# A fused two-layer kernel, its last chunk: pair 0 gated and row 1 turned earlier, pair 2's gates mixed by ScalarE and VectorE, and a third outer product on GpSimd

## The reference

```python
x = layernorm(x + L0_attn(x))
x = layernorm(x + L0_ffn(x))     # silu(x w1) * (x w2), two gelu layers of 1024, w3
x = layernorm(x + L1_attn(x))    # k, v, q = x W; k over its block norms; per step a state
                                 #   S = tanh(S + outer(v - S k, k)), out = f(S q), f(z) = z^2 sigmoid(z)
x = layernorm(x + L1_ffn(x))     # xr = mu_r x + (1 - mu_r) x_prev, xk likewise with mu_k
                                 #   out = sigmoid(xr W_r) * (relu(xk W_k)^2 W_v)
```

## Time and profile before

| | |
|---|---|
| timed runs, median | 1147.56 us |
| the profiled execution | 1148.24 us |
| its span in the profile | 1146.3 us |
| TensorE busy | 1096.8 us (96%) |
| VectorE busy | 954.2 us (83%) |
| ScalarE busy | 596.7 us (52%) |
| GpSimd busy | 516.8 us (45%) |

### The profile page before, as it was taken

One profiled execution on the slowest core, in us unless ns is written; L12 is line 12 of the kernel. 1 busy time (PEld: TensorE's weight loads), 2 busy tenths in 40 slices (PEclk: granted clock), 3 DMA queues, 4 the chain that ended last, 5 costly groups with the idle time before them and its releaser, 6 DMA issues.

```text
span 1146.3 us, 16623 instructions
## 1 busy us (share of the span) xinstructions
PE 1096.8 (96%) x5837; PEld 850.3 (74%) x5837; DVE 954.2 (83%) x1382; ACT 596.7 (52%) x1009; POOL 516.8 (45%) x426
## 2 busy tenths in 40 slices
PE   9999999999999999999999999999999999998386
PEld 5566666678787777788778887877887787886165
DVE  4798888882045998999899899989989998999886
ACT  2345555554446346645755574565557455644534
POOL 1477666774333244433424432443343344337852
PEclk9999999999999999999999999999999999999679
DMA  7246555523532430523134133314232330430001
GB/s 265 102 167 236 211 204 209 222 93 114 179 94 58 145 110 21 146 74 129 56 110 138 46 110 91 128 39 126 77 124 73 110 128 19 129 92 20 0 1 39
DMA packets 45114, 127.01 MB, mean 111 GB/s; under 512 B 4352, under 2 KB 21504, under 8 KB 43136
## 3 DMA queue, kind: packets, MB, share of 16 engines
q1 hardware_dynamic: 43904, 114.20, 31.5%
q10 hardware_dynamic: 1152, 12.07, 2.8%
HBM read 117.86 MB, written 19.92 MB: 120 GB/s over the span
## 4 chain that ended last, share of the span: by engine, by line
PE 77%; DVE 12%; POOL 6%; issue 3%; ACT 2%; POOLq 0%; DVEq 0%; ACTq 0%
PE lower L1257 46%; PE bank L1257 18%; PE lower L440 5%; PE lower L572 2%; POOL state L748 2%; POOL rgn L757 2%; PE bank L1246 1%; DVE y L847 1%; DVE y L852 1%; PE bank L487 1%; POOL a_lo L2017 1%; DVE tmp L2265 1%; PE lower L526 1%; PE lower L530 1%; PE bank L440 1%
## 5 line engine op out<-in xcount | busy, mean ns | idle before, releaser
L2017 POOL TENSOR_TENSOR a_lo<-whole,a_hi 128x512 fp32r<-128x512 f32 x128 | 181.9, 1438 | 267.0 <-ACT a_hi L1629 195.7
L1257 PE MATMUL lower<-b_hi,ring 128*128 128x512 f32 x512 | 193.6, 396 | 1.4 <-ACT a_hi L1629 1.4
L1257 PE MATMUL lower<-b_lo,ring 128*128 128x512 f32 x512 | 190.6, 390 | 1.7 <-POOL b_lo L2017 1.7
L1257 PE MATMUL lower<-a_hi,ring 128*128 128x512 f32 x496 | 186.3, 394 | 1.7 <-issue 1.7
L1257 PE MATMUL lower<-a_lo,ring 128*128 128x512 f32 x496 | 184.1, 389 | 0.3 <-POOL a_lo L2017 0.3
L2017 POOL TENSOR_TENSOR b_lo<-whole,b_hi 128x512 fp32r<-128x512 f32 x64 | 93.5, 1469 | 145.4 <-ACT b_hi L1629 145.4
L1612 ACT ACTIVATE S<-S 128x1024 f32<-128x1024 f32 x56 | 58.6, 1058 | 173.5 <-DVE S L2278 173.5
L1628 ACT ACTIVATE whole<-lower,hs 128x512 f32<-128x512 f32 x126 | 86.2, 685 | 79.3 <-PE lower L1257 77.3
L1257 PEld LDWEIGHTS lower<-b_hi,ring 128*128 128x128 f32 x512 | 96.2, 188 | 22.0 <-issue 1.8
L1257 PEld LDWEIGHTS lower<-b_lo,ring 128*128 128x128 f32 x512 | 96.0, 188 | 22.0 <-POOL b_lo L2017 2.3
L440 PE MATMUL lower<-wa,xT 128*128 128x512 f32 x240 | 109.5, 599 | 1.5 <-DVE turned L817 1.4
(11 more groups left out here) (302 smaller groups left out, 2398.9 us busy)
## 6 DMA issues: line engine op xcount, KB each, us to landing
ring<-ffn_copy_dram SPq DMA_DIRECT2D x128, 512.0 KB, 3.6
look<-ffn_dram ACTq DMA_DIRECT2D x6, 1879.0 KB, 6.9
ffn_copy_dram<-ffn_dram SPq DMA_DIRECT2D x4, 2112.0 KB, 11.4
rope<-rope_dram SPq DMA_DIRECT2D x8, 512.0 KB, 8.2
xtok<-x_dram SPq DMA_DIRECT2D x8, 512.0 KB, 4.2
x1in<-x_dram SPq DMA_DIRECT2D x8, 512.0 KB, 4.8
x1res<-x_dram SPq DMA_DIRECT2D x8, 512.0 KB, 3.3
xT<-xT_dram SPq DMA_DIRECT2D x7, 512.0 KB, 8.4
```

The source lines that it names most:

```text
L1257: ins = nc.tensor.matmul(out, a, b, start=(first and n == 0), stop=(last and n == len(pairs) - 1))
L2017: nc.gpsimd.tensor_tensor(lo[:, m, :], t["whole"][:, m % 4, :], hi[:, m, :].bitcast(F32), ALU.subtract).then_inc(lo_done, 1)
```

## The change

All of it is in the four `finish()` programs and their helpers.

- GpSimd takes a third outer product, that of s = 0. VectorE's `next_state(0, 1)` becomes `state_delta(0)`, then `scaled_keys(2, ...)`, then `state_added(0)`. `outer_product(0)` stands ahead of `read_q(0, 0)`; `mix_weights(3)` goes behind the reads of s = 0; `read_q(3, 0)` goes ahead of `added_mean(1)`.
- VectorE: `read_sums(0)` goes behind `next_state(1, 0)`, `mixed_pair(0)` ahead of `state_delta(2)`, `gate_rows(front)` ahead of `state_added(2)`, `mixed_pair(1)` behind `last_read(1)`. `update_sum` loses its reduce to `update_state` and, as `update_times`, goes behind the third of the rows.
- Pair 2's gates are made from mixed inputs (`mixed_gates`): two more copies on ScalarE, two more mixes on VectorE (`last_mix_inputs(0)`), four products instead of eight on TensorE.
- Rows: the fourth `last_down` goes ahead of `turn_row(0)`, ScalarE copies row 1 before its tanh, and `busy_while_waiting` runs six products at two places instead of eight at one.

```diff
-            READS = {(0, 0): 1, (0, 1): 2, (1, 0): 3, (1, 1): 4, (2, 0): 6, (2, 1): 7, (3, 0): 9}
-            OUTERS = {1: 5, 2: 8}
+            READS = {(0, 0): 2, (0, 1): 3, (1, 0): 4, (1, 1): 5, (2, 0): 7, (2, 1): 8, (3, 0): 10}
+            OUTERS = {0: 1, 1: 6, 2: 9}
...
+                        if g == 2:
+                            mixed_gates(n, gates, 1)
+                            return
...
+                    def mixed_gates(n, gates, mixed):
+
+                        pe.wait_ge(last_mixed, mixed)
+                        for r, b in enumerate(range(2 * n, 2 * n + 2)):
+                            ins = product(gates[:, r * DIM:r * DIM + DIM],
+                                          [(wide_b[:, k, b * P:b * P + P], wr[:, k, :]) for k in range(KD)])
+                        ins.then_inc(pair_dr, 1)
...
-                    for b in range(3):
+                    for b in range(BATCH):
                         last_down(b)
                     turn_row(0)
-                    last_down(3)
                     key_value_row(0)
                     query_row(0)
+                    pe.wait_ge(sig_done, 2 * LAST - 2)
+                    busy_while_waiting(bank[KEY_BANK[1]], 6)
...
-                    busy_while_waiting()
+                    pe.wait_ge(pair_sig, 2)
+                    busy_while_waiting(pair_banks(2)[1], 6)
...
                     x2_rows(1, range(1, BATCH))
+                    turned_row(1)
                     scan_tanh(d, BATCH - 1, 1)
-                    for b in range(1, BATCH):
+                    for b in range(2, BATCH):
                         turned_row(b)
...
+                    last_parts(2, 0)
                     key_acts(2, 0)
                     mix_gates(2, 0)
...
                     x2_root(1, slice(1, BATCH))
                     key_root(0, slice(0, 1))
-                    mix_weights(3)
                     key_root(1, slice(1, 2))
                     added_mean(0, every)
                     key_root(2, slice(2, BATCH))
                     added_root(0, every, t["rstd4"], t["shift4"])
+                    outer_product(0)
                     read_q(0, 0)
                     read_q(0, 1)
+                    mix_weights(3)
...
                     outer_product(2)
+                    read_q(3, 0)
                     added_mean(1, front)
-                    read_q(3, 0)
...
+                    ffn_row(1)
+                    ffn_row(2)
+                    update_times(d, 3, 1)
+                    ffn_row(3)
...
                     next_state(0, 0)
-                    next_state(0, 1)
+                    state_delta(0)
                     scaled_keys(2, slice(2, BATCH))
+                    state_added(0)
+                    next_state(1, 0)
                     read_sums(0)
-                    next_state(1, 0)
                     state_delta(1)
                     read_sums(1)
                     state_added(1)
                     next_state(2, 0)
+                    mixed_pair(0, 0)
                     state_delta(2)
                     read_sum(2, 0)
-                    mixed_pair(0, 0)
+                    gate_rows(front, 2, 1)
                     state_added(2)
-                    gate_rows(front, 2, 1)
-                    mixed_pair(1, 1)
                     read_sum(2, 1)
                     read_sum(3, 0)
                     last_read(1)
+                    mixed_pair(1, 1)
                     gate_rows(back, 6, 2)
+                    last_mix_inputs(0)
```

More of the change, by code:

```diff
@@ L1517, in last_products, with busy_while_waiting @@
                         ins.then_inc(pair_dk, 1)
-                        pe.wait_ge(last_mixed, 2)
                         pe.wait_ge(pair_gated, g)
-                        for r, b in enumerate(rows):
-                            ins = product(gates[:, r * DIM:r * DIM + DIM],
-                                          [(wide_b[:, k, b * P:b * P + P], wr[:, k, :]) for k in range(KD)])
-                        ins.then_inc(pair_dr, 1)
-                    def busy_while_waiting():
-                        pe.wait_ge(pair_sig, 2)
-                        for _ in range(8):
-                            nc.tensor.matmul(pair_banks(2)[1][:, 0:DIM], ident[:], wk[:, 0, :], start=True, stop=True)
+                        mixed_gates(n, gates, 3)
+                    def busy_while_waiting(unused, count):
+                        for _ in range(count):
+                            nc.tensor.matmul(unused[:, 0:DIM], ident[:], wk[:, 0, :], start=True, stop=True)
                     def pair_values(g, n):
@@ L1870, in last_parts @@
                         act.wait_ge(pair_dv, g - 1)
-                        for dst, nu in ((wide_a, nu_k), (wide_b, nu_r)):
+                        for dst, nu in ((wide_a, nu_k), (wide_b, nu_r))[3 - g:]:
                             for k in range(KD):
@@ L2104, in outer_product @@
                         pool.wait_ge(fin_times_k, DELTAS[s])
-                        if s == 2:
+                        if s:
                             pool.wait_ge(fin_pre, 2 * s + 2)
@@ L2255, in update, with update_times @@
                 def update(c, s, hf):
-                    update_sum(c, s, hf)
+                    update_times(c, s, hf)
                     update_state(s, hf)
-                def update_sum(c, s, hf):
+                def update_times(c, s, hf):
                     k, v, q, st, w = parts(s, hf)
-                    dl = delta[:, hf * HALF:hf * HALF + HALF, :]
                     dve.wait_ge(sq_done, c * 2 * BATCH + 2 * (s - 1) + hf + 1)
                     scan.done(nc.vector.tensor_tensor(w, st, along_j(k), ALU.mult))
-                    scan.wait()
-                    scan.done(nc.vector.tensor_reduce(dl, w, AX_X, ALU.add))
                 def update_state(s, hf):
@@ L2272, in update_state @@
                     dl = delta[:, hf * HALF:hf * HALF + HALF, :]
+                    scan.wait()
+                    scan.done(nc.vector.tensor_reduce(dl, w, AX_X, ALU.add))
                     scan.wait()
@@ L2569, in finish @@
                     row_moments(fin, t["mv2"], slice(0, 1), ve2)
-                    update_sum(d, 3, 1)
-                    for b in range(1, BATCH):
-                        ffn_row(b)
+                    ffn_row(1)
+                    ffn_row(2)
+                    update_times(d, 3, 1)
+                    ffn_row(3)
                     row_moments(fin, t["mv2"], slice(1, BATCH), ve2)
```

17 lines of the change are left out of this document (8 added, 9 removed).

## The result

The changed kernel took 1152.06 us (median of seven runs, 1150.85 to 1152.23) against 1147.56 (1147.28 to 1148.2): ratio 1.0037, interval 1.0027 to 1.0047. It is slower by 4.2 us by the ratio, 4.5 by the medians. The profiled executions took 1152.09 and 1148.24, with spans of 1150.3 and 1146.3. The last chunk begins 0.27 us later than before (`ffn_row(0)` at 1045.24 instead of 1044.97). No edit explains that; over the fourteen traces of this case `ffn_row(0)` starts between 1044.82 and 1045.38, so differences of this size are not counted as anybody's effect.

The account below looks back on a forecast made before the run. VectorE's chain of states bounds the last chunk to about 1115, then a relay of VectorE, ScalarE, GpSimd and TensorE. Back gates +2.7 and mixes +0.8 make +3.5, on the median 1147.56: 1151.1 us, range 1148.8 to 1154.0.

Parts of the forecast that it names:

- outer product ends: GpSimd's third outer product, started only after the fourth key root and added_root at 1081.77: ends 1083.8 to 1085.0, taken as 1084.5.
- back gates: Gates of pair 1's rows on VectorE, after last_read(1) and ScalarE's last gate parts: 1128.4 instead of 1125.74, +2.7 us.
- The lock: VectorE operation with two SBUF inputs and GpSimd operation reading SBUF exclude each other: the later starts when the earlier ends.
- The milder lock: Rival: front gates get their second turn before read (3,0), or first read ends before sums need it; -1.8, 1149.3; 12%.
- rivals without a lock: Rival: no lock at state_added(0) and the reads beside it; next_state(1, 0) starts at 1087.1, total 1144.0 us; 4%.
- fixed price of 0.6: Rival: each meeting of VectorE and GpSimd costs 0.6; four new meetings on the path, 2.4 us, total 1146.4; 4%.
- read_sums moved: Sums of step 0 placed behind next_state(1, 0): later GpSimd reads land on VectorE's operations, state_added(1) at 1104.7, +4.6 us.
- The rows: Row edits up to the start of step 1: -0.5 us, from 1074.16 to 1073.65; bounds 0 and 1.6.
- The half clock in rows 2 and 3: TensorE at 1.2 GHz in these rows after idling: ScalarE's sums, and with them GpSimd, up to 1.2 us later.
- Pair 2's gates: Two added mixes on VectorE's path cost +0.8 us; TensorE's saved 1.8 of 3.62 us is worth nothing, through at 1133.2.
- the slow clock: Rival: TensorE at 1.2 GHz at pair 2, keys up to 6.6 instead of 3.7 us, late by 2.2 to 3; 1153.7; 15%.
- 3.90 us wait: VectorE's wait before 1118.89 for TensorE's values of pair 1: goes away, giving back 2.6 us.

Follow-up runs that it names:

- short_reads: Changed kernel with GpSimd's two reads of step 0 cut to one block of sixteen each, all waits and signals kept: 1147.51 us, ratio 0.9999.
- one_input: Changed kernel with one SBUF operand of state_added(0) exchanged for the old contents of the PSUM array: 1150.41 us, ratio 1.0025.
- rows_only: Kernel before with the row edits alone, including mix_weights(3) behind the reads of step 0: 1147.71 us, ratio 1.0003.
- no_mixed: Changed kernel with pair 2's gates as before the change, eight products and no mixes: 1153.58 us, ratio 1.0048.
- fill9: Changed kernel with nine unused filler products instead of six ahead of pair 2: 1151.37 us, ratio 1.0037.
- no_outer: Changed kernel without the third outer product, read_sums(0) ahead of next_state(1, 0) again: 1147.27 us, ratio 0.9996.
- sums_first: Changed kernel with read_sums(0) moved back ahead of next_state(1, 0), third outer product kept: 1149.3 us, ratio 1.0013.
- mix3_back: Changed kernel with mix_weights(3) back ahead of the second key root on GpSimd: 1151.35 us, ratio 1.0032.
- best3: best2 with 24 fillers right behind pair 1's values, and ScalarE's last half-state tanh and row 2 gate parts moved earlier: 1147.88 us, ratio 1.0002.
- gates_late: Changed kernel with the front gates behind state_added(2) and read (3, 0) behind added_mean(1) again: 1152.58 us, ratio 1.0045.
- best: Changed kernel without third outer product; both last q products on VectorE, second sum of step 2 ahead of state_added(2), front gates behind it: 1146.03 us, ratio 0.999.
- best2: best with the first sum of step 0 ahead of the keys-and-norms product, and ScalarE's row 3 gate parts ahead of pair 2's copy: 1146.01 us, ratio 0.9985.

## Why the prediction was right, step by step

The forecast was 1151.1 with a range of 1148.8 to 1154.0, slower with 76%; it came to 1152.06. The mechanism and the chain of states came as predicted; the last step, pair 2, did not, and that the sum is off by only 1 us is in part luck, as two errors of opposite sign met. The terms, as times and as shifts against the kernel before (the 0.27 us of the later start is in the measured ones):

| place | forecast | measured |
|---|---|---|
| step 1 starts | 1073.65 | 1073.29 |
| outer product ends | 1084.5 | 1084.36 |
| next_state(1, 0), its product ends | +1.0 | +0.56 |
| state_added(1) | 1104.7, +4.6 | 1104.44, +4.3 |
| second front gate ends | 1120.8 | 1120.30 |
| last_read(1) | 1124.5, +2.0 | 1123.72, +1.25 |
| back gates | 1128.4, +2.7 | 1128.14, +2.4 |
| VectorE's rows for pair 3 ready | +3.5 | +3.1 |
| transposes of pair 3 | 1133.9, +3.5 | 1134.52, +4.1 |

*The lock.* Right in mechanism and size. The add, the products and the gates waited whole operations; short_reads and one_input show that it is GpSimd's reads, and the count of SBUF inputs. The milder lock is out too: read (3, 0) came between the two gates. The rule of the Trainium skill that the prediction cited ("SBUF — State Buffer", section "Who interferes with whom") holds in both: one SBUF input, 1.23 us beside a read; two, 3.28. The lock "for the whole instruction" was not met at two places where GpSimd's operation has one input (last section). The rivals without a lock and with a fixed price of 0.6 are out: 3.28 less 1.22 is 2.06.

*read_sums moved.* I put 3.6 of the 4.6 us at `state_added(1)` on it. Moved back alone it gave 1.6, or 2.4 at equal starts; with it, the second sum waits 1.12 for read (0,1) and next_state(1, 0) starts at 1091.89. The two moves are not additive: whichever stands first, VectorE waits for both of GpSimd's reads, once in longer operations and once in idle time. Undoing the outer product gave back all 4.3.

*The rows.* I took 0.5 us for the start of step 1; it was 0.87. Neither enters the sum, for the outer product was counted from GpSimd's chain (1081.77 before, 1081.96 after). As a gain of their own the row edits are none, shown by rows_only. The half clock in rows 2 and 3, which I had in the bounds as up to 1.2 us, costs 0.6 at the start of step 1 in the five traces that have it.

*Pair 2's gates.* The one step that failed. I wrote that TensorE would be through at 1133.2 and its saving worth nothing. That took 3.7 us for the keys; they took 5.41, and TensorE was late by 1.1 us. So in this trace VectorE's 0.8 for the mixes was wholly hidden, and the four products left out save 1.7 (no_mixed). "Worth nothing" was wrong at full clock too, by my own figures: with eight products TensorE would have been through at 1127.6 + 3.7 + 3.6 = 1134.9, a microsecond behind VectorE's 1133.9. In fill9, at full clock, the gates start at 1130.77; with eight products, which take 3.46 us from there to the transposes in no_mixed (1132.46 to 1135.92), these would come at an estimated 1134.2 instead of 1133.16. I had missed that pair 2's keys start 4.1 us later than before (1127.55 instead of 1123.42), more than VectorE's back gates, so that TensorE would be the late one without the saving. The sum was not touched by that, since it has the mixes in. I had given the slow clock 15% as a rival, and its price as 2.2 to 3; it happened at half the price or less, for the keys took 5.41 and not 6.6. The smaller terms before it took off 0.4, the clock put 1.1 on top: +4.1 in the trace instead of +3.5. The other 0.4 between this and the 4.5 of the medians comes from laying a difference of traces on a median: the profiled execution before took 0.68 more than its median, the one after 0.03 more.

*What the 3.90 us wait gave back.* It is gone, as forecast. VectorE is busy 22.09 of 22.40 us in the third window.

What stays open: the level of the clock at pair 2 from run to run. Of the profiled executions, it was full in the keys of pair 2 in no_outer, rows_only, sums_first, short_reads, one_input, mix3_back, fill9 and best3, and half in the changed kernel, no_mixed, gates_late, best and best2. The traces separate by what TensorE did between the fillers and the transposes of pair 2: it was idle for 1.17 to 1.55 us in the five with half clock, and for 0.24 us or nothing in the eight with full clock. That goes together in all thirteen, and in the kernel before; which is the cause of which isn't shown, as the fillers themselves are longer when they run at half clock and then close the gap. What it is worth: 1.7 us in the keys, of which 1.1 reached the transposes in the changed kernel, as much as some of the edits that were being measured.

## What to carry to other kernels

Before giving GpSimd work that VectorE does, list VectorE's operations with two SBUF inputs in the same stretch: each pays the rest of the GpSimd operation it meets, and GpSimd's next one may come first. Sums with one input, or an operand in PSUM, can stand there for nothing; the version that put a sum into such a wait was 1.1 us earlier at that place by it. And an edit that frees VectorE gains only until the next operation that waits for GpSimd's queue.

## What the runs showed of the hardware that I had not expected

- GpSimd's operations with one array from SBUF (and a scale per partition) wait too. The two `mixw<-wr,nu_r` took 2.80 us in the changed kernel, where VectorE's product ran until 1091.04, and 1.83 where VectorE made a sum (the version with the sums first). The other way round the wait was not seen: VectorE's product with two SBUF inputs started inside the second of them and took 1.28 us at 1091.89 in sums_first (`mixw` until 1092.53) and 1.22 at 1087.86 in best2 (until 1088.40). So "the later starts when the earlier ends" is shown for GpSimd operations with two inputs, not for every one.
- TensorE's granted clock fell in the middle of the fillers, not only after a wait. In the run without the outer product it was 1.00 until 1118, through 2.6 us of idling, and then:

```profile
1118.00:1121.00 3.00, 3.00 (x8) 2.37 (x8) 2.94 (x4) 1.58 (x4) 2.04 (x3) 0.50 0.00 0
```

  There the fillers took the slow part (4.54 us for twelve rows) and the keys had 3.72. In the changed kernel the fillers ran at 1.00 (2.86 us) and the keys got the slow part. In gates_late both were slow, fillers 4.54 and keys 5.41, with 1.17 us of idling between fillers and transposes. The same six fillers are worth 1.7 us or nothing.
